# A graph network kernel on one Trainium2 core: the semaphores and refills of two gather rings go from groups of eight columns to quads of four

## The reference, cut to what matters

```python
h = x @ W1 + b1
h_i, h_j = h[dst], h[src]
e = jnp.concatenate([h_i, h_j - h_i], axis=-1)
m = relu(e @ W2 + b2)
m = relu(m @ W3 + b3)
out = relu(segment_max(m, dst, num_segments=6250))
x = layernorm(x + out)
# then two graph attention layers (softmax over the edges of each node),
# relu after each, and a second layernorm(x + ...)
```

## Time and profile before

| | |
|---|---|
| median of 3 runs | 5763.31 us |
| runs, lowest to highest | 5754.06 to 5776.48 us |
| span of the profiled execution, first to last instruction | 5744.4 us |
| PE, PEld, DVE, ACT, POOL busy | 77%, 67%, 71%, 48%, 38% of the span |
| granted clock of TensorE, mean over the span | 0.863 |
| edge stage | 212 to about 2970 us |

### The profile page before, as it was taken

How to read it: one execution, slowest core, us unless ns; L and a number is a source line. 1 busy time by engine, 2 the same in 40 slices (tenths; PEclk the granted TensorE clock), 3 DMA queues, 4 the chain that set the end, 5 groups by cost and what they waited for, 6 DMA issues and landing times.

```text
span 5744.4 us, 99002 instructions
## 1 busy us (share of the span) xinstructions
PE 4395.5 (77%) x35974; PEld 3827.1 (67%) x35974; DVE 4053.4 (71%) x6352; ACT 2772.7 (48%) x3925; POOL 2154.4 (38%) x2116
## 2 busy tenths in 40 slices
PE   4388878778778787887855848889887848888884
PEld 2266666666666666666644638888886637888884
DVE  4255555555555565555636949999996949999998
ACT  1033333333333333333322029999994009999996
POOL 4765556556566665665651030011111030001111
PEclk9677878788888888888877969999998979999997
DMA  4356555556566665665552622122221632112221
GB/s 133 110 167 171 165 160 165 166 159 170 161 172 171 178 176 169 170 172 172 171 151 97 230 66 61 57 60 66 62 64 52 230 114 52 57 57 69 60 63 50
DMA packets 764462, 717.37 MB, mean 125 GB/s; under 512 B 97095, under 2 KB 632703, under 8 KB 764152
## 3 DMA queue, kind: packets, MB, share of 16 engines
q1 hardware_dynamic: 424822, 319.77, 18.6%
q10 hardware_dynamic: 271394, 258.61, 16.0%
q0 software_dynamic: 67936, 135.03, 8.5%
HBM read 536.76 MB, written 176.36 MB: 124 GB/s over the span
## 4 chain that ended last, share of the span: by engine, by line
PE 29%; DVE 23%; issue 22%; another core or an unknown queue 14%; ACT 8%; ACTq 2%; POOL 1%; DMA 0%; SPq 0%; DVEq 0%; POOLq 0%
DVE ring_b L1250 13%; PE ps L1455 10%; DVE work L1239 5%; PE ps L1428 5%; PE ps L1418 5%; PE ps L1438 2%; PE ps L1417 2%; ACT ring_a L707 2%; PE ps L1583 2%; ACT work L786 1%; DVE work L1146 1%; ACT tab_flat L676 1%; ACT work L783 1%; POOL P_compact L578 1%
## 5 line engine op out<-in xcount | busy, mean ns | idle before, releaser
L557 POOL DMA_INDIRECT ring_a<-Q_table,late x1563 | 1648.1, 1054 | 1096.7 <-PE ps L1418 534.1
L1583 PE MATMUL ps<-tab_flat,ring_b 128*128 128x129 f32 x12152 | 1488.8, 280 | 77.4 <-DVE ring_b L1250 74.9
L1583 PEld LDWEIGHTS ps<-tab_flat,ring_b 128*128 128x128 f32 x12152 | 1424.8, 195 | 119.8 <-DVE ring_b L1250 117.7
L1035 DVE TENSOR_TENSOR_SCAN work<-ring_b,work,ps 128x512 f32<-128x512 bf16 x391 | 498.4, 1275 | 1042.6 <-remote 761.5
L1455 PEld LDWEIGHTS ps<-work,tab_flat 128*128 128x128 bf16 x7936 | 790.4, 143 | 605.9 <-issue 584.0
L1455 PE MATMUL ps<-work,tab_flat 128*128 128x49 bf16 x7936 | 900.2, 273 | 319.8 <-ACT ring_a L707 220.2
L1239 DVE TENSOR_TENSOR work<-work 128x1024 f32<-128x1024 f32 (+1 forms) x784 | 931.1, 1188 | 115.2 <-ACT work L786 111.7
L783 ACT ACTIVATE work<-work,scores 128x1024 f32<-128x1024 f32 (+1 forms) x784 | 879.5, 1122 | 133.8 <-DVE ring_b L1250 108.3
L1250 DVE SCALAR_TENSOR_TENSOR ring_b<-work,ring_a 128x1024 f32<-128x1024 f32 (+1 forms) x784 | 928.9, 1185 | 2.1 <-PE ps L1583 1.9
L786 ACT ACTIVATE work<-work,slope_src 128x1024 f32<-128x1024 f32 (+1 forms) x784 | 868.0, 1107 | 0.0
L707 ACT ACTIVATE ring_a<-ps 128x490 uint8<-128x490 f32 x806 | 469.3, 597 | 823.9 <-remote 432.0
(11 more groups left out here) (247 smaller groups left out, 4748.3 us busy)
## 6 DMA issues: line engine op xcount, KB each, us to landing
work<-P_compact SPq DMA_DIRECT2D x1563, 64.0 KB
work<-low_rows SPq DMA_DIRECT2D x312, 320.0 KB, 3.7
ring_b<-rank_rows ACTq DMA_DIRECT2D x194, 512.0 KB
run_max<-tab_flat ACTq DMA_DIRECT2D x194, 512.0 KB
ring_a<-counts SPq DMA_DIRECT2D x98, 896.0 KB, 5.0
counts<-ring_a ACTq DMA_DIRECT2D x62, 784.0 KB
ring_a<-Q_table,late POOLq DMA_INDIRECT x1563
ring_a<-counts SPq DMA_DIRECT2D x14, 672.0 KB, 4.3
```

The source lines that it names most:

```text
L557: pool.indirect_dma_start(out=q_ring[:, g % RING, j - j0, :], out_offset=None, in_=Q_table, in_offset=bass.IndirectOffsetOnAxis(ap=srcT_i[ ...
L1583: m = tensor.matmul(sums_of(tau), lhsT=a_ring[:, u % RINGA, (tau - a) * P:(tau - a + 1) * P], rhs=tab[:, h, 0:F + 1], start=(h == 0 and (t ...
```

## The change: what it does

Each slot of the two rings gets two semaphores, one for each quad (half) in it: four transfers raise each. PE's `place(i)` waits for its own half alone. POOL and SP wait for `placed` once for each half, for the quad six before (the same half of group g - 3), and then issue that half's four transfers. Number, size and order of the transfers within each queue stay as they are, and the slots stay as large.

The six more semaphores come out of ones that are merged elsewhere: pairs that are raised and waited for a few times in the whole program now share one with a higher value (`cf_padded` and `lf_padded`; `ends_made` and `live_made`; `high_listed` and `low_listed`; `link_spread` and `base_spread`; `tail_made` and `shift_made`; `tail_spread` and `shift_turned`).

```diff
-        q_value = totals([g % RING for g in range(NG)], [16 * (j1 - j0) for g, (j0, j1) in enumerate(groups)])
-        w_value = totals([g % RING for g in range(NG)], [16 * (j1 - j0) for g, (j0, j1) in enumerate(groups)])
+        in_half = [(g % RING, a // 4) for (g, a, n) in quads]
+        q_value = totals(in_half, [16 * n for (g, a, n) in quads])
+        w_value = totals(in_half, [16 * n for (g, a, n) in quads])
+        quad_of = {(g, a): i for i, (g, a, n) in enumerate(quads)}
...
-        q_landed = [sem(f"q_slot{i}") for i in range(RING)]
-        w_landed = [sem(f"w_slot{i}") for i in range(RING)]
+        q_landed = [[sem(f"q_slot{i}_half{h}") for h in range(2)] for i in range(RING)]
+        w_landed = [[sem(f"w_slot{i}_half{h}") for h in range(2)] for i in range(RING)]
...
             def load_windows(g, column, free):
-                if g >= RING:
-                    sync.wait_ge(placed, free)
                 for a in range(0, j1 - j0, 4):
                     n = min(4, j1 - j0 - a)
+                    if g >= RING:
+                        sync.wait_ge(placed, free + a // 4 + 1)
...
-                        sync.dma_start(w_ring[:, slot, a + i, :], P_compact[bass.ds(at[i], P), :]).then_inc(w_landed[slot], 16)
+                        sync.dma_start(w_ring[:, slot, a + i, :], P_compact[bass.ds(at[i], P), :]).then_inc(w_landed[slot][a // 4], 16)
...
-                    load_windows(RING + p, column + p * G, free + 2 * (p + 1))
+                    load_windows(RING + p, column + p * G, free + 2 * p)
...
             def gather_q(g):
                 j0, j1 = groups[g]
-                if g >= RING:
-                    pool.wait_ge(placed, last_of[g - RING] + 1)
                 for j in range(j0, j1):
+                    half, first = divmod(j - j0, 4)
+                    if g >= RING and first == 0:
+                        pool.wait_ge(placed, quad_of[g - RING, 4 * half] + 1)
...
-                tensor.wait_ge(q_landed[g % RING], groups_done(q_value[g]))
-                tensor.wait_ge(w_landed[g % RING], groups_done(w_value[g]))
+                tensor.wait_ge(q_landed[g % RING][a // 4], groups_done(q_value[i]))
+                tensor.wait_ge(w_landed[g % RING][a // 4], groups_done(w_value[i]))
...
-                count, groups_done = grows(ROUND), grows(16 * G)
+                count, groups_done = grows(ROUND), grows(16 * 4)
```

More of the change, by code:

```diff
@@ L340, in edge_network @@
         runs_stored = [sem(f"run_rows{i}") for i in range(2)]
-        cf_padded, zeros_made, consts_made, blanks_made, lf_padded = (
-            sem(n) for n in ("cf_padded", "zeros_made", "consts_made", "blanks_made", "lf_padded"))
+        ends_padded, zeros_made, consts_made, blanks_made = (
+            sem(n) for n in ("ends_padded", "zeros_made", "consts_made", "blanks_made"))
         hist_hot, hist_done, cnt_made, counted, rows_made = (
@@ L350, in edge_network @@
         pq_made, p_added, q_copied = sem("pq_made"), sem("p_added"), sem("q_copied")
[L351 to L354, removed]
+        rows_counted, ends_made, starts_made, place_made = (
+            sem(n) for n in ("rows_counted", "ends_made", "starts_made", "place_made"))
+        path_made, link_made, link_spread, src_listed = (
+            sem(n) for n in ("path_made", "link_made", "link_spread", "src_listed"))
         att_turned, att_t_copied, att_made, att_copied = (
@@ L365, in edge_network @@
             sem(n) for n in ("bias_ended", "proj_turned", "proj_copied", "proj_made", "proj_att", "proj_tab"))
-        scores_split, low_made, picked, topped, tops_turned, tail_made, tail_spread, shift_made, shift_turned, tops_run = (
-            sem(n) for n in ("scores_split", "low_made", "picked", "topped", "tops_turned", "tail_made", "tail_spread",
-                             "shift_made", "shift_turned", "tops_run"))
+        scores_split, low_made, picked, topped, tops_turned, tail_made, tail_spread, tops_run = (
+            sem(n) for n in ("scores_split", "low_made", "picked", "topped", "tops_turned", "tail_made", "tail_spread", "tops_run"))
         sides_made, sides_turned, sides_copied, window_spread, window_hot_made, window_copied = (
@@ L379, in sync_program @@
         def sync_program(sync):
-            sync.wait_ge(cf_padded, 1)
+            sync.wait_ge(ends_padded, 1)
             whole = L // P
@@ L438, in sync_program @@
                 for p in range(RING):
-                    load_windows(RING + p, column + p * G, free + 2 * (p + 1))
+                    load_windows(RING + p, column + p * G, free + 2 * p)
             for g in range(RING * ROUNDS, NG):
-                load_windows(g, groups[g][0], last_of[g - RING] + 1)
+                load_windows(g, groups[g][0], quad_of[g - RING, 0])
             low_value = totals([g % RINGX for g in range(NX)] * 2, [16] * (2 * NX))
@@ L941, in vector_program @@
             vector.tensor_copy(end_i[:, :], s["s0"][:, :]).then_inc(dve.up(), 1)
-            vector.tensor_scalar(s["cnt"][:, :], s["empty"][:, :], -1.0, 1.0, ALU.mult, ALU.add).then_inc(live_made, 1)
+            vector.tensor_scalar(s["cnt"][:, :], s["empty"][:, :], -1.0, 1.0, ALU.mult, ALU.add).then_inc(ends_made, 1)
             vector.wait_ge(dve.sem, dve.n)
@@ L1015, in vector_program @@
             vector.wait_ge(dve.sem, dve.n)
-            vector.tensor_copy(low_sb, src_ints).then_inc(low_listed, 1)
+            vector.tensor_copy(low_sb, src_ints).then_inc(src_listed, 1)
             def spread_ranks(i):
@@ L1397, in tensor_program @@
             tensor.wait_ge(path_made, 2)
-            tensor.matmul(ps[1][:, 256:256 + NT], lhsT=ident[:, 0:1].to_broadcast([P, P]), rhs=v["s0"][:, :], start=True, stop=True).then_inc(base_spread, 1)
+            tensor.matmul(ps[1][:, 256:256 + NT], lhsT=ident[:, 0:1].to_broadcast([P, P]), rhs=v["s0"][:, :], start=True, stop=True).then_inc(link_spread, 1)
             tensor.wait_ge(q_copied, -(-NB // 2))
```

33 lines of the change are left out of this document (16 added, 17 removed).

## The result

The changed kernel takes 5518.85 us (median of four runs, 5507.19 to 5527.27) beside 5769.9 us of the kernel before (median of four runs made with them). The ratio is 0.957, with a 95% interval of 0.954 to 0.961: 4.3% faster, some 250 us. The forecast was 5701 us, with a range from 5575 to 5840 us.

A forecast was written before the change was run, and what follows sets the result against it. PE bounds the edge stage, held up by its own late signals during refills, not by landing transfers. Refills 59 us plus head 3 us, other terms 0, took 5763 to 5701 us; range 5575 to 5840 us.

The forecast's parts named there:

- the signs that were named: Edge stage: POOL's waits twice as many and shorter, stage about 60 us shorter, relu waiting less, clock at least 0.82.
- the clock: PE's clock in the edge stage: 27 us per 0.01 of its mean, left out of the sum, widening the range downwards.
- The waits by halves at place: PE waiting per half slot at place: 0 in the steady state, because slots land two groups ahead.
- The earlier start of a refill and the larger lead: Ring refills: first half starts one quad earlier, about 7 us; lead grows from 16 columns to 20; worth 0.
- The head of the stage: PE's first place in the edge stage starts between 0 and 6.1 us earlier; 3 us taken.
- The merged semaphores: Semaphores waited for outside the edge stage's loop: 0, at most a few tenths of a us either way.
- Added waits: One more wait a group on POOL and SP: 0 on the path, as both have slack.
- The refills by halves: POOL's and SP's refills in the edge stage, four transfers per placed quad: a gain of 59 us.
- the hole at PE: PE's idle time late in a long refill: bounds of 176 us gain or loss, a third of the gain taken.
- The cause behind the hole: Edge stage: PE's signals reach others late during refills of eight gathers; PE runs dry after about 8 us.
- Rival B: Edge stage: a late signal for every quad makes it slower, 5851 us at half the 176 us loss; chance 0.25.
- Rival A: Edge stage: nothing moves, signals late as often as now, 5760 us; chance 0.28.

The follow-up runs named there:

- e3: Changed kernel with POOL's gathers and SP's window loads both refilled by groups again; semaphores by halves and PE's half-slot wait kept: 5741.28 us, ratio 0.997.
- e5: Changed kernel, but PE waits at a slot's first quad for all eight gathers and loads: 5525.2 us, ratio 0.962.
- e4: Changed kernel, refills still by halves but each started one quad later: 5527.22 us, ratio 0.959.
- e19: The changed kernel itself, run in the last series, where the kernel before took 5027.73 us: 5056.92 us, ratio 1.006.
- e9: e3 with SP's eight window loads starting one quad after POOL's eight gathers: 5545.85 us, ratio 0.976.
- e15: Changed kernel without SP's window loads from the fourth group on, gathers by halves: 5497.74 us, ratio 0.953.
- e17: e15 with POOL's gathers by groups of eight again: 5556.36 us, ratio 0.962.
- e1: Changed kernel with POOL's gathers by groups of eight again, SP still loading by halves: 5667.85 us, ratio 0.984.
- e10: Changed kernel with every gather replaced by a plain load of 128 consecutive rows from the same queue: 4877.3 us, ratio 0.860.
- e6: e3 without the gathers of Q rows from the fourth group on, window loads kept: 4884.27 us, ratio 0.851.
- e14: Changed kernel with every gather still indexed, but by a list of consecutive rows: 5513.45 us, ratio 0.955.
- e18: Changed kernel with SP's half loads waiting for multiplied in place of placed, run in the last series: 5091.2 us, ratio 1.012.

## Why the prediction was wrong

**The direction and the place were right.** All but 2.5 us of the gain lies in the edge stage, and PE's signals are late there. Of the signs that were named, POOL's waits became more and shorter (119 to 192 in 1800 us, 418 to 296 us), the relu waited less, and the clock rose; but the stage ended not 60 us earlier but 236.

**The waits by halves at place, 0:** right (e3, e5). **The earlier start of a refill and the larger lead, 0:** right (e4). **The head of the stage, 3 us:** PE's first place stands at 220.4 us after the change, 218.27 before, while the stage before it differs too; the 3 us can't be told. **The merged semaphores, 0:** right within e3's 0.3%. **Added waits, 0:** nothing contradicts it; even in e19, where POOL sets the pace, its pauses are no longer for them.

**The refills by halves, 59 us: this step failed, in two terms.** First the hole at PE: its bound was 176 us and I took a third. PE's time without work fell by 130 us, three quarters of the bound. My reason for a third was that POOL rests only 1.9 us between bursts so that signals stay late. They do stay late (86 relus for 89, 392 raises for 389), but less so: the relus wait 2.1 us each instead of 4.0, and the pipeline carries more of that. The third itself was a choice that no row gave. Second the clock: I worked out 27 us for 0.01 of its mean and then put it at nothing in the sum, with no reason given. It rose by 0.04, which gives 108 us, and PE's busy time fell by 106. In place of 59 us the two terms measured 130 + 106 = 236 us, the stage's gain. The range's low end had the whole hole in it but just 9 us for the clock. The rule on back-to-back matmuls that I had cited from the Trainium skill (Perfetto Trace Analysis, Matmul Optimizations) as paying twice agrees with the trace: smaller holes (559 to 429 us) and a higher clock (0.82 to 0.86) came together.

**The cause behind the hole was half seen.** I laid it to the length of a burst of gathers. e9 and e15 to e17 point to long bursts of gathers meeting bursts of window loads as the larger part. I had given SP's halves nothing; they bring 1.3 points by themselves (e1).

**Rival B, slower,** had its place right (signals late at every quad) and its price wrong: shorter lateness, not more cases. **Rival A** comes nearest to what happened in the last series, where signals weren't late and the change brought nothing.

## What to carry to other kernels

When a supplier refills a ring long ahead of its consumer, look at how its bursts fall beside the work, not only at whether they land in time: here the same transfers in pieces of four instead of eight gave 4.3% though no engine waited for them to land. When a hole at TensorE is expected to shrink, put the clock into the sum with it; here it was as large a term as the hole. And measure the kernel before beside every series of runs: it ran at 5760 and at 5028 us, and the change's sign went with it.

## What the runs showed of the hardware

- TensorE's semaphores can be raised late, 2 us after its last matmul in the mean and up to 11.7 us (kernel before), while POOL issues indexed transfers in runs; those of ACT and DVE are not (0.01 us). With the same bytes as plain loads from the same queue (e10), or with no gathers (e6), PE's come after 0.01 us, the clock is 1.00 from 700 to 2000 us, and the kernel takes 4877 to 4884 us: 788 us less than the kernel before in e10's series (5665 - 4877), halves included. Consecutive indices don't help (e14, 0.955).
- In the last series (e18, e19) the indexed transfers ran without any late signal, POOL at 11.0 us for eight. What decides it is open.
- A wait of POOL that has already passed adds nothing that can be seen to the pause between two gathers, 0.3 us at its longest in 700 to 2000 us of e19.
- A plain load cost POOL 547 ns in e10 where a gather costs 1050.
